# A two-layer graph network on one core: table picks masked by VectorE instead of by a TensorE matmul

## The reference

```
p1   = (x @ W_lin + b_lin) @ W1_agg                       # per node, 16 features
h1   = tanh(mean over incoming edges of p1[src] + root + b1)
x1   = layernorm(x + tanh(mean of h1[src] @ W2_agg + h1 @ W2_root + b2))
hn   = x1 @ Wn.T + bn                                      # per node, 64 features
w    = ssp(ssp(edge_attr @ We1.T + be1) @ We2.T + be2)     # per edge
agg  = segment_sum(hn[src] * w, dst)
out  = layernorm(x1 + ssp(agg @ Wc.T + bc) @ Wp.T + bp)
```

## Time and profile before

| what | value |
|---|---|
| median of 3 runs | 9696.16 us (9692.97 to 9697.18) |
| time of the profiled execution | 9691.73 us |
| its span, first to last instruction | 9690.0 us |
| mean granted TensorE clock | 0.874 |
| TensorE (matmul) busy | 7374.5 us, 76% |
| VectorE busy | 5759.0 us, 59% |
| ScalarE busy | 4850.6 us, 50% |
| GpSimd busy | 6802.9 us, 70% |

### The profile page before, as it was taken

How to read it: one execution, slowest core, us unless ns; L and a number is a source line. 1 busy time by engine, 2 the same in 40 slices (tenths; PEclk the granted TensorE clock), 3 DMA queues, 4 the chain that set the end, 5 groups by cost and what they waited for, 6 DMA issues and landing times. The chain is left out here.

```text
span 9690.0 us, 147348 instructions
## 1 busy us (share of the span) xinstructions
PE 7374.5 (76%) x45123; PEld 6762.7 (70%) x45124; DVE 5759.0 (59%) x6867; ACT 4850.6 (50%) x8146; POOL 6802.9 (70%) x6954
## 2 busy tenths in 40 slices
PE   6999999888889999998888754444444445666665
PEld 6999999888889999998888633333333334555554
DVE  4666676777656666676677544444444444555555
ACT  3666666555546666665555243434343433333343
POOL 4777777765537777777666377777777777777774
PEclk9999999999989999999999777777777777888887
DMA  3111121111111122221111122222222222222221
GB/s 76 47 48 49 49 49 46 42 39 38 38 32 49 49 49 48 47 49 40 38 38 38 33 52 51 53 50 54 50 54 50 54 50 54 50 54 50 54 50 36
DMA packets 391376, 459.65 MB, mean 47 GB/s; under 512 B 196464, under 2 KB 258631, under 8 KB 390804
## 3 DMA queue, kind: packets, MB, share of 16 engines
q0 software_dynamic: 220000, 164.28, 10.1%
q1 hardware_dynamic: 169378, 294.14, 9.6%
q10 hardware_dynamic: 1938, 0.49, 0.0%
HBM read 448.12 MB, written 10.27 MB: 47 GB/s over the span
## 5 line engine op out<-in xcount | busy, mean ns | idle before, releaser
L610 PE MATMUL banks<-split_sb,e_low_hot 128*128 128x400 f32 x20000 | 4280.6, 358 | 39.5 <-ACT e_low_hot L580 39.5
L610 PEld LDWEIGHTS banks<-split_sb,e_low_hot 128*128 128x128 f32 x20000 | 3793.6, 192 | 85.1 <-ACT e_low_hot L580 40.0
L808 POOL DMA_INDIRECT big<-hn_table,src_i x3125 | 3099.5, 992 | 958.5 <-issue 947.9
L555 POOL DMA_INDIRECT big<-p_table,src_i x1875 | 1805.5, 963 | 753.2 <-issue 559.7
L555 POOL DMA_INDIRECT big<-h_table,src_i x1875 | 1807.1, 964 | 730.5 <-issue 556.6
L580 ACT ACTIVATE e_low_hot<-e_key_off 128x1536 fp32r<-128x1536 f16 x1000 | 1272.2, 1272 | 1852.1 <-PE banks L613 1821.0
L576 ACT ACTIVATE e_key_off<-e_key_in,node_off 128x384 f16<-128x384 f16 (+1 forms) x4000 | 1920.8, 551 | 113.8 <-DMA e_hi_in<-sel_dram 32.2
L682 DVE SCALAR_TENSOR_TENSOR hot<-dst_f,win_base,banks 128x1536 bf16<-128x1536 f32 (+1 forms) x934 | 1762.6, 1896 | 305.5 <-issue 187.1
L662 DVE TENSOR_REDUCE picked<-banks 128x48 f32<-128x1200 f32 x1000 | 1195.1, 1195 | 1206.8 <-PE banks L613 1204.1
L826 PE MATMUL banks<-e_wide,we 128*128 128x512 f32 x1000 | 630.9, 800 | 1442.3 <-DVE e_wide L922 1432.7
L826 PEld LDWEIGHTS banks<-e_wide,we 128*128 128x128 f32 x1000 | 287.9, 303 | 1723.9 <-DVE e_wide L922 1512.0
(11 more groups left out here) (187 smaller groups left out, 3837.6 us busy)
## 6 DMA issues: line engine op xcount, KB each, us to landing
e_wide<-in_edge_t SPq DMA_DIRECT2D x125, 832.0 KB, 4.5
e_key_in<-sel_dram SPq DMA_DIRECT2D x250, 320.0 KB
e_hi_in<-sel_dram SPq DMA_DIRECT2D x250, 320.0 KB
big<-hn_table,src_i POOLq DMA_INDIRECT x3125
big<-p_table,src_i POOLq DMA_INDIRECT x1875
big<-h_table,src_i POOLq DMA_INDIRECT x1875
src_i<-in_src SPq DMA_DIRECT2D x375, 12.5 KB, 1.7
x<-in_x SPq DMA_DIRECT2D x1, 3136.0 KB, 11.0
```

The lines of the kernel that those rows point to most:

```text
L555: pool.indirect_dma_start(buf[u][:, j, 0:ROW0], None, table, bass.IndirectOffsetOnAxis(ap=src_i[u][:, j:j + 1], axis=0),).then_inc(gathere ...
L610: pe.matmul(o, low_hot[gr][:, h, e], split_sb[:, h:HI1 * HI2:HI2, part * H:(part + 1) * H], start=(h == 0 and part == 0), stop=False)
L808: pool.indirect_dma_start(buf[u][:, j, 0:F], None, table, bass.IndirectOffsetOnAxis(ap=src_i[u][:, j:j + 1], axis=0),).then_inc(gathered[u ...
```

## The change

- The ninth matmul of each slot and everything that serves it is gone: `others`, `hi_hot`, `hi_in` with its DMA, `hi_key`, `hi_made`. Each slot has eight matmuls.
- VectorE makes a small mask for each block, `high` (10 slots by 25 candidates, `high_hots`), from the high digits that the setup now leaves in SBUF (`sel_hi`).
- `take` is two instructions: a multiplication of the group's candidates in PSUM by the mask, into `masked` in SBUF, then a drain, then a sum over the 25 candidates. `masked` is laid out so that the 25 numbers of a sum lie side by side. `pick_taken` is counted up by the multiplication.
- Five groups of two slots on three sets of banks (0, 2, 4, 0, 2). TensorE does groups 0 and 1 of the next block ahead of the visits and groups 2, 3, 4 behind them.
- VectorE makes both one-hots of a window inside the visit's loop, for the current window only.
- The setup makes 10 transposes instead of 20.

The diff, cut to its core:

```
-SIZE = (3, 2, 3, 2)
+SIZE = (2, 2, 2, 2, 2)
-AT = (0, 3, 5, 8)
-BANK0 = (0, 3, 0, 3)
+AT = (0, 2, 4, 6, 8)
+BANK0 = (0, 2, 4, 0, 2)
+TAKEN = (1, 2, 2, 3, 4)
...
                     def pick(gr, n):
                         pe.wait_ge(low_made, NGR * n + gr + 1)
-                        pe.wait_ge(hi_made, NGR * n + gr + 1)
-                        pe.wait_ge(pick_taken, NGR * n + gr + 1)
+                        pe.wait_ge(pick_taken, NGR * n + TAKEN[gr])
                         for k in range(SIZE[gr]):
...
                                 for part in range(2):
-                                    pe.matmul(o, low_hot[gr][:, h, e],
-                                              split_sb[:, h:HI1 * HI2:HI2, part * H:(part + 1) * H],
-                                              start=(h == 0 and part == 0), stop=False)
-                            last = pe.matmul(o, hi_hot[gr][:, e], others[:, :, :], start=False, stop=True)
+                                    last = pe.matmul(o, low_hot[gr][:, h, e],
+                                                     split_sb[:, h:HI1 * HI2:HI2, part * H:(part + 1) * H],
+                                                     start=(h == 0 and part == 0), stop=(h == HI2 - 1 and part == 1))
...
-                                pe.wait_ge(hot_made[h], visit + 1 + (n if h == 0 else 0))
+                                pe.wait_ge(hot_made[h], visit + 1)
...
                         if inside(n + 1):
                             pick(0, n + 1)
+                            pick(1, n + 1)
                         add_up(n, g, u)
                         if inside(n + 1):
-                            pick(1, n + 1)
-                            pick(2, n + 1)
-                            pick(3, n + 1)
+                            for gr in range(2, NGR):
+                                pick(gr, n + 1)
...
-                    def high_hots(gr, turn, u):
-                        es = slice(AT[gr] * P, (AT[gr] + SIZE[gr]) * P)
-                        if gr == 0:
-                            dve.wait_ge(keys_in[u], 32 * turn)
-                        dve.tensor_scalar(hi_hot[gr][:, :], hi_in[u][:, es], hi_key[:, :], None,
-                                          ALU.is_equal).then_inc(hi_made, 1)
+                    def high_hots(n, u):
+                        dve.tensor_tensor(high[u % 2][:, :, :],
+                                          sel_hi[:, bass.ds(n, 1), :].rearrange("p o j -> p (o j)").unsqueeze(2)
+                                          .to_broadcast([P, SEL, HI1]),
+                                          iota_row[:, 0:HI1].unsqueeze(1).to_broadcast([P, SEL, HI1]), ALU.is_equal)
+                        dve.drain()
...
-                        dve.tensor_reduce(picked[:, AT[gr]:AT[gr] + SIZE[gr], :], found, AX.X,
-                                          ALU.max).then_inc(pick_taken, 1)
+                        mine = high[u % 2][:, AT[gr]:AT[gr] + SIZE[gr], :].unsqueeze(2).to_broadcast(
+                            [P, SIZE[gr], H, HI1])
+                        dve.wait_ge(pick_psum, NGR * n + gr + 1)
+                        dve.tensor_tensor(m, found, mine, ALU.mult).then_inc(pick_taken, 1)
+                        dve.drain()
+                        dve.tensor_reduce(picked[:, AT[gr]:AT[gr] + SIZE[gr], :], m, AX.X, ALU.add)
...
                         since, to, first = windows(dve, n, True)
-                        make_hot(0, n, 0, since + 1)
-                        take(3, n)
-                        if inside(n + 1):
-                            high_hots(3, turn_of(g, u + 1), (u + 1) % 2)
+                        take(NGR - 1, n, u)
                         parts(u)
                         with dve.Fori(since, to) as visit:
...
+                            make_hot(0, n, window, visit + 1)
                             make_hot(1, n, window, visit + 1)
-                            make_hot(0, n, window + 1, visit + 2)
...
                         if inside(n + 1):
-                            for gr in range(3):
-                                take(gr, n + 1)
-                                if inside(n + 2):
-                                    high_hots(gr, turn_of(g, u + 2), u % 2)
+                            high_hots(n + 1, u + 1)
+                            for gr in range(NGR - 1):
+                                take(gr, n + 1, u + 1)
```

75 lines of the change are left out of this document (27 added, 48 removed).

## The result

The changed kernel takes 9863.84 us (median of 4 runs, 9862.21 to 9865.25) against 9694.56 us for the kernel before (4 runs, 9692.36 to 9697.18): a ratio of 1.0174 with a 95% interval of 1.0157 to 1.0192, or 169 us more. The forecast was 9758 us, 62 us above the 9696.16 us that it started from: the right direction, and the result lies just inside the range of 9670 to 9870 us, but the forecast has hardly more than a third of the loss. The profiled execution's span is 9860.5 us.

What follows compares the result with a forecast made beforehand. Gathers (19.0 us) were taken to bound one-window blocks, TensorE two-window ones. One-window unchanged, two-window 23.8 to 24.5 us (+63 us), setup -2: span 9751, forecast 9758 us; own range 9725 to 9800 (chance 0.50), overall 9670 to 9870.

Steps and rivals of the forecast that it cites:

- The bound of the one-window blocks: GpSimd's 15 gathers set one-window blocks at 19.0 us, against TensorE 17.1 and VectorE 18.8 after the change: no change.
- The prices of the new instructions: On VectorE: multiplication 0.99 us, sum 0.99, a whole `take` 1.98, mask 0.42 (0.5 with its drain).
- the gap of the reads: Reading `visits` into registers between take 3's sum and take 4: 2.3 instead of 0.9 us, 1.4 lost on VectorE.
- The whole one-window chain: VectorE's line of work from the end of one TensorE visit to the end of the next: 18.7 us.
- 0.1 for the loop's branch every fourth block: Added to VectorE's 18.7 us chain for the loop coming round, giving 18.8 us.
- 0.2 more because TensorE's short visit after a pause is often at half its clock: Added to a two-window block's 24.3 us for a half visit of 1.41 instead of 0.9 us: 24.5 us.
- The third rival: VectorE overtakes GpSimd in one-window blocks too, perhaps with TensorE's clock lowered by pauses: +92 us, 9850 us; chance 0.23.
- the forecast's own signs of being wrong: Two-window blocks under 23.8 us, or the first pass's one-window stretch longer than 1475 us.
- VectorE's share near 70%: Sign of being right: VectorE's busy share, 59% before, would be near 70% in the changed kernel.
- The first rival: `visits` reads hidden or chain otherwise 1.4 us shorter: two-window blocks 23.1 us, -63 us, 9631 us; chance 0.12.
- the second: Chain somewhat shorter, ending where the old one did: two-window blocks at 23.8 us, 9694 us; chance 0.15.
- The rule about the port: Removing `hi_hot` may free GpSimd's descriptor writing on the port shared with VectorE: at most 0.1 us a block, left out.

Runs made afterwards that it cites:

- the run with the pauses filled: Changed kernel plus throwaway matmuls on TensorE, 6 and 3 ahead of its waits for the two one-hot halves of each visit: 9773.23 us.
- the fastest version: Changed kernel with the three `visits` reads taken apart and the next existing window's first one-hot made before the sums are added: 9493.69 us.

## Why the forecast of the loss was too small

**The bound of the one-window blocks: right for the kernel before, wrong by 0.14 us for the changed one.** Taking 1.9 us of TensorE's work out of each block gained nothing, and once VectorE is shorter the gathers hold a block at 18.9. But the changed kernel's 19.0 us is VectorE's: one gather less leaves it there. The forecast put VectorE's 18.8 beside the gathers' 19.0 and saw no difference. It should have put it beside 18.86: the gathers do need 1.265 us each, 19.0 a block, but block 0's end 10.6 us ahead of their visit in the changed kernel (12.6 before), and the visits may use up this lead over 78 blocks, which lets them come every 18.86 us. At 19.00 the changed kernel uses up none of it.

**The prices of the new instructions: right** to 0.02 us each, and the gap of the reads to 0.1. The whole one-window chain, forecast at 18.7 us from visit to visit, is 18.71 in the trace.

**"0.1 for the loop's branch every fourth block": too small by 0.2.** The mean over the stretch is 19.00, not 18.8. About half of the difference is the branch, with its gap of 1.70 instead of 1.27 us. The other half is TensorE's half clock: in 10 of 74 blocks from 200 to 1615 us take 3 or take 4 waits for TensorE's slots, which take 16.1 to 16.8 us there, and these blocks are 19.5 us long (1072.83 to 1092.32). In the run with the pauses filled no such block is left.

**"0.2 more because TensorE's short visit after a pause is often at half its clock": this is the step that failed.** It took one row, a half visit of 1.41 instead of 0.9 us, and halved it. It left out the slots behind that visit, which are at half clock too. The sum without this term, 24.3 us, was good: 24.4 is what the run with the pauses filled gives for blocks without half clock. The clock's part of the 25.5 us is therefore about 1.1 us, not 0.2. The fillers took 0.8 of it away, and the rest is an estimate. It was the right mechanism at a fifth of its size: 0.9 us x 90 blocks is 81 of the 106 us that the forecast lacks, and the one-window blocks' 0.14 x 156 are 22.

The price could have been read in the trace before. Beside the row of 1.41 us stands a block of 24.4 us, and beside a half visit of 0.86 us one of 23.0. So an episode of half clock cost 1.5 us even behind a pause of 1.76 us, about half of the blocks had one, and the new chain was to lengthen this pause to about 3 us in each (0.3 for the sum, 0.6 round the loop, 1.9 for a one-hot). The mean of 23.8 us was no full-clock figure either. At full clock a two-window block goes from 23.0 to about 24.4 us by these rows, so, as an estimate, most of the loss of 1.7 us is VectorE's chain without the overlap, and some 0.3 is that there is more half clock than before.

**The third rival** named both parts of what happened, VectorE's chain above the gathers' pace and a clock that falls in the pauses, but placed the clock in the one-window blocks. There TensorE's pauses are mostly 0.75 to 1.05 us and the clock stays at 0.99; it is the second window's pause of 2.96 us that brings most of the half clock. Its 9850 us is near the measured 9864 by luck: it is 0.3 us for each one-window block, where 0.14 came, and 0.5 on top of the forecast for each two-window block, where 1.0 came. That the result lies within the overall range is owed to this rival's share in it, and not to the forecast's sum.

**The signs.** Two of the forecast's own signs of being wrong came true or nearly so: the one-window stretch took 1482 us (wrong from 1475 on), and two-window blocks are 25.5 us apart (24 to 25 was right). VectorE's share near 70% was a slip: the forecast's own instructions add up to about 500 us on top of 5759 us, which is 64% of its 9751 us, and 64% is what the profile shows. ScalarE's busy time did not stay as before. It rose by 263 us, from 4850.6 to 5113.9, since its elements are cut into 25% more instructions. That cost nothing here: TensorE waits for it for 36 us in the whole run.

**What the change lost it with.** Read part by part: the one-hots only for visited windows save VectorE 1.95 us in every block. In a two-window block they take away the overlap of a one-hot with TensorE's visit, and putting it back brings 2.7 us. The new picks with that overlap kept are 1.0% faster than the kernel before, and with the reads apart 2.1%. That the reads' gap by itself costs 1.3 us of VectorE but returned 0.6 fits the same reading: at half clock TensorE's slots were as late as VectorE.

**The first rival** (reads hidden, or a chain 1.4 us shorter) and **the second** (two-window blocks at 23.8 us) are out: the gap is in each block's timeline.

**The rule about the port.** The `hi_hot` instructions left VectorE's list, and the mean of a gather in the one-window stretch went from 962 ns to 960. By the Trainium skill, SBUF — State Buffer, section "Who interferes with whom", such instructions can hold GpSimd up. A difference of 2 ns is too little to show that they did.

**Left open.** What is left of the clock's part when the fillers' 0.8 us is taken off, some 0.3 us, is not shown by a run of its own: in the block in four that keeps its half clock, fillers lie in TensorE's way too. Whether the kernel before would gain from the loss of L613 alone, or from the overlapped order alone, was tried only on chips where it ran at 13,190 us.

## What to carry to other kernels

When an edit removes work that "nobody uses", look in the timeline for what that work ran beside: here it was the reason why a one-hot was ready before the sums were added, and a conditional start of the next window keeps both. And when a summed chain leaves TensorE a new pause, price the clock for what comes behind the pause, not for one matmul group: here 3 us of pause made the next 25 matmuls up to twice as long and the next ten slots 1 to 2 us longer. Look first whether the trace before has blocks of both kinds, with and without half clock, as it had here (24.4 and 23.0 us): the difference is the price.

After an engine is relieved, ask at once what is next in line (gathers at 18.9 us, slots at half clock): it, and not the relieved engine's saving, sizes the gain.

## What the runs showed of the hardware

The half clock came with a pause of TensorE of 2.96 us between two short visits. When 1.3 us of filler matmuls stood in that pause it went from most blocks, although TensorE still waited 1.72 us after them. Shorter pauses did not rule it out: in the kernel before it came behind about half of the pauses of 1.76 us, and in the changed kernel behind one of 1.30 us. Pauses of 0.75 to 1.05 us, two for each block of 18.7 us, left the stretch's clock at 0.99. In the fastest version a visit's 25 matmuls behind waits for the last gather to land take 2.03 and 2.24 us instead of 1.58; but with the reads taken apart there is one of 1.56 us behind a wait of 1.68. So the length of the last pause alone does not say in these runs whether half clock follows.

```profile
1006.55 2.03 PE L608 MATMUL banks<-hot,big 128*64 128x128 bf16 x25 [2.42 <-DMA big<-p_table,src_i]
...
1044.33 2.24 PE L608 MATMUL banks<-hot,big 128*64 128x128 bf16 x25 [1.96 <-DMA big<-p_table,src_i]
```

Adding 3,078 matmuls to TensorE's list made the kernel 80 to 91 us faster, the spread being that between the two chips.

Three register reads of VectorE in one run, with a drain ahead of the next operation, stopped it for 1.27 us (1.70 in every fourth block); the same three, each with an operation of 0.99 us to lie beside, for not more than 0.15 us (1.06 us from the start of a 0.99 us sum to the next multiplication, instead of 0.91).

The same program took 13,190 instead of 9,690 us on another chip, with eight matmuls at full clock still at 1.68 us and TensorE stopping between them. A comparison there has another bound and says little of the kernel at 9,690 us.
